# Edge stage's first microseconds: VectorE converts the row numbers first, ScalarE clears the sums

## What is computed

```python
h = relu(u[row] + v[col])
mask = sigmoid(h @ W2 + b2)
sum_w[row]  += mask                 # segment sums over the edges
sum_wx[row] += mask * x[col]
agg = sum_wx / (sum_w + 1e-9)
```

## Time and profile before

| | us |
|---|---|
| time, median of 3 runs | 4230.29 (4230.21 to 4234.32) |
| the profiled execution's own time | 4232.93 |
| its span, first to last instruction | 4231.2 |
| GpSimd's gathers L1706, busy in the span | 1089.1 in 1088 instructions |
| VectorE / TensorE / ScalarE / GpSimd busy in the span | 2994.9 / 3503.2 / 2188.8 / 1547.7 |

### The profile page before, as it was taken

The page is one execution under the profiler, slowest core; times in us unless marked ns, Lnnn a source line. Parts: engine busy times, 40 slices in busy tenths (PEclk is TensorE's granted clock), DMA queues, the critical chain, the costliest instruction groups (busy, mean ns, idle before and its releaser), DMA issues. The chain is left out here.

```text
span 4231.2 us, 94148 instructions
## 1 busy us (share of the span) xinstructions
PE 3503.2 (83%) x20637; PEld 2391.9 (57%) x20638; DVE 2994.9 (71%) x11952; ACT 2188.8 (52%) x6957; POOL 1547.7 (37%) x1256
## 2 busy tenths in 40 slices
PE   5878882698889899995997898688888888888884
PEld 2377772333333344443445344588888888888873
DVE  8899987698888888885003002688888888787875
ACT  2178884266677788884002001455555555555544
POOL 0078874000000000001002001377777777777770
PEclk8855555699999999997999999899999999999996
DMA  2011113001111222221983885355555555555551
GB/s 49 1 11 15 15 17 84 10 35 44 62 70 79 88 97 96 96 90 65 328 303 131 313 304 189 123 151 153 153 151 151 150 150 149 149 150 149 151 147 41
DMA packets 276478, 498.31 MB, mean 118 GB/s; under 512 B 92441, under 2 KB 192944, under 8 KB 276256
## 3 DMA queue, kind: packets, MB, share of 16 engines
q1 hardware_dynamic: 209922, 347.11, 24.4%
q0 software_dynamic: 66336, 149.10, 13.0%
HBM read 391.18 MB, written 104.89 MB: 117 GB/s over the span
## 5 line engine op out<-in xcount | busy, mean ns | idle before, releaser
L1706 POOL DMA_INDIRECT xs<-edge_table,ea_row_stage x1088 | 1089.1, 1001 | 347.4 <-issue 326.1
L1257 PE MATMUL a_agg_ps<-a_adj_ring,parts 128*128 128x512 f16 (+1 forms) x2548 | 523.7, 369 | 46.1 <-DMA a_adj_ring<-adjacency 46.1
L1926 ACT ACTIVATE slot_dst<-ea_onehot,ea_mask 128x128 f32<-128x128 f16 x1632 | 535.7, 399 | 13.2
L1056 PE MATMUL ab_agg_ps<-ab_adj_stage,parts 128*128 128x512 f16 x1911 | 528.2, 387 | 0.0
L1880 PE MATMUL ea_psz<-parts,ea_onehot_t 128*128 x2176 | 309.2, 287 | 206.6 <-issue 188.5
L1920 ACT ACTIVATE ea_mask<-ea_dot,b 128x4 f32<-128x4 f32 x408 | 121.3, 297 | 676.6 <-DVE slot_src L1831 672.9
L441 POOL DMA_INDIRECT records<-both_parts,record_row x98 | 356.1, 3633 | 291.0 <-ACT both_parts L467 269.1
L1397 POOL TENSOR_TENSOR parts<-xs,parts 128x896 f16<-128x896 f32 x7 | 13.2, 1883 | 1225.1 <-ACT parts L1391 1225.1
L1891 PE MATMUL ea_psa<-xs,slot_dst 128*128 128x129 f32 x3264 | 438.6, 278 | 2.4 <-ACT slot_dst L1926 2.4
L1129 ACT ACTIVATE ab_src_off<-iota,ab_neg_src 128x128 f16<-128x128 f16 x712 | 282.2, 396 | 304.8 <-issue 141.2
L1257 PEld LDWEIGHTS a_agg_ps<-a_adj_ring,parts 128*128 128x128 f16 x2548 | 242.2, 98 | 327.8 <-DMA a_adj_ring<-adjacency 47.0
(11 more groups left out here) (391 smaller groups left out, 6455.8 us busy)
## 6 DMA issues: line engine op xcount, KB each, us to landing
a_adj_ring<-adjacency SPq DMA_DIRECT2D x182, 896.0 KB, 4.6
ea_low_rows<-low_rows SPq DMA_DIRECT2D x411, 128.0 KB
adjacency<-ab_adj_stage SPq DMA_DIRECT2D x91, 512.0 KB, 2.6
adjacency<-ab_adj_stage SPq DMA_DIRECT2D x91, 384.0 KB, 2.3
ea_near_rows<-near_rows SPq DMA_DIRECT2D x137, 128.0 KB
xs<-edge_table,ea_row_stage POOLq DMA_INDIRECT x1088
edge_table<-vx SPq DMA_DIRECT2D x12, 512.0 KB, 2.9
ea_row_stage<-row_columns SPq DMA_DIRECT2D x272, 2.0 KB, 1.8
```

The costliest lines, as they stand in the source:

```text
L1056: ins = nc.tensor.matmul(agg_ps[:, :], lhs(r, t), stage[:, k, :], start=start and r == 0, stop=stop and r == parts - 1)
L1257: ins = nc.tensor.matmul(ps[:, h, 0:width], lhs(r, t), ring[:, g % SLOTS, k * DB:k * DB + width], start=t == 0 and r == 0, stop=t == NT - ...
L1706: nc.gpsimd.indirect_dma_start(got[:, h, g, k, 0:ROW], None, m.table, bass.IndirectOffsetOnAxis(ap=row_s[:, h, g, k:k + 1], axis=0)).then_ ...
L1926: ins = nc.scalar.activation(hot_m[:, g, k, :], hot[:, h, g, :, k], ACT.Copy, scale=mask[:, g, k:k + 1])
```

## The change

VectorE now begins with the conversion of the column numbers (L1770 to L1772 of before) and the copies to `row_s`; the two buffers of ones, `lo16` and the wait for `s_ones` come behind the copies, ahead of the first one-hots. The clearing of `m.acc` leaves VectorE: ScalarE writes it as its first instruction of the stage, as a copy of a zero row that is broadcast over the 49 tiles, and that instruction adds the 16 to `s_add`. VectorE's first addition of turn 1 now waits for `s_add` too. `lo16` is followed by a wait for its completion.

```diff
         @block.vector
         def _(dve):
             ch = Chain(dve, s_v)
-            nc.vector.memset(m.acc[:, :, :], 0.0)
-            dve.sem_inc(s_add, 16)
-            nc.vector.memset(near_x[:, :, :], 1.0)
-            nc.vector.memset(got[:, :, :, :, ROW:ROW + 4], 1.0).then_inc(s_ones, 1)
-            nc.vector.tensor_copy(lo16[:, :], m.slot_src[:, 0:SCP])
             ai = m.slot_dst[:, SCP:2 * SCP].bitcast(I32)
             ch(nc.vector.tensor_copy(ai, m.slot_dst[:, 0:SCP]))
             ch(nc.vector.tensor_scalar(ai, ai, SPAN - 1, None, ALU.bitwise_and))
             ch(nc.vector.tensor_scalar(row_of, ai, float(NP - 1), None, ALU.min))
             dve.sem_inc(s_table, 1)
-            dve.wait_ge(s_ones, 2)
...
                 if q == 0:
                     dve.wait_ge(s_agg[g], t)
-                if seen >= 2 or g or q:
-                    dve.wait_ge(s_add, t * 6 + (g * 2 + q + 10))
+                dve.wait_ge(s_add, t * 6 + (g * 2 + q + 10))
...
             stage_rows(base[0:2], 0)
             stage_rows(base[4:6], 1)
+            nc.vector.memset(near_x[:, :, :], 1.0)
+            nc.vector.memset(got[:, :, :, :, ROW:ROW + 4], 1.0).then_inc(s_ones, 1)
+            ch(nc.vector.tensor_copy(lo16[:, :], m.slot_src[:, 0:SCP]))
+            dve.wait_ge(s_ones, 2)
             one_hots(base, 0, 0, 0)
...
+            nc.scalar.activation(m.acc[:, :, :], m.zeros16[:, 0:AW].unsqueeze(1).broadcast_to([P, NT, AW]), ACT.Copy).then_inc(s_add, 16)
             act.wait_ge(s_ones, 2)
             turns(act, step)
```

## The result

| | us |
|---|---|
| the changed kernel, median of 14 runs | 4226.08 (4218.87 to 4231.18) |
| the kernel before, measured beside it, median of 14 | 4232.6 (4224.47 to 4240.76) |
| ratio | 0.9981 (0.9973 to 0.9990), or -8.0 us (-11.4 to -4.2) |
| the profiled execution, and its span | 4226.97, 4225.3 |

The forecast was 4223.0, that is 7.3 us less than the median of the three runs of before that were known then; the measured median lies 3.1 us above it, inside the range. Of these 3.1 us, 2.3 are the kernel before itself, whose median is 4232.6 in 14 runs where it was 4230.29 in three. The medians lie 6.5 us apart, the means 7.9, and the ratio gives 8.0.

What follows compares the result with a forecast made beforehand. GpSimd's unbroken line of gathers bounds the stage, with VectorE's preamble bare ahead of it. 8.03 us of earlier start less 0.7 for lengthened gathers gives 7.3 us, from median 4230.29 to 4223.0; range 4218.8 to 4227.8.

Steps and rivals of the forecast that it cites:

- The line of gathers as the bound: GpSimd issues 1088 gathers one behind another over 1423.2 us; moving the first gather moves the end by as much.
- At a fixed distance: What follows the last gather of the stage was said to follow it at an unchanging distance.
- VectorE's start at 2688.40: VectorE is free at 2688.40, before its memset's row at 2689.68, so L1770 at 2696.43 can start 8.03 us earlier.
- late-start rival: The 1.4 us ahead of VectorE's memset are a real delay that L1770 would suffer too; gain 6.0 us, chance 0.12.
- Kept as it is: 3.14 us: VectorE's conversions L1770 to L1772 keep their 3.14 us; from L1770 to the first gather are 5.52 us.
- The lengthened gathers: VectorE's work beside the first four gathers stretches them from 4.68 to 5.32 us; 0.7 us of loss taken.
- The covers: ScalarE's clearing costs nothing, with 10 us of cover; VectorE's 4.32 us idle before first scores shrinks by about 1 us.
- The sign that would have made the forecast wrong: A gap before a gather of turn 2 showing a releaser other than "issue"; no size of gap given.
- Unlengthened gathers: Rival: the first four gathers run at 0.96 us each; gain 8.9 us, time 4221.4, chance 0.14.
- A new wait before turn 2: Rival: crowded transfers delay landings by 3 us and GpSimd's line stops for 1.5; gain 5.8 us, chance 0.12.
- Another releaser of the first gather: Rival: something other than VectorE's copies released the first gather, only about 1 us moves; 4229 us, chance 0.02.
- Slower through another phase of the loop: Rival: VectorE's one-hots fall on other gathers all loop; at 0.12 us more a turn, 4239.3 us, chance 0.04.

Runs made afterwards that it cites:

- the clearing alone: The kernel before with only the clearing of the sums moved to ScalarE, VectorE's other work in its old order; -6.4 +- 3.2 us against the kernel before.
- order-alone kernel: The changed kernel, but the clearing stays on VectorE, behind the copies and ahead of the first one-hots; -4.5 +- 3.5 us against the kernel before.
- the longer front: The kernel before with the clearing memset done four times, all ahead of the copies; two runs, +12.1 +- 3.5 and +17.4 +- 4.9 us against the kernel before.

## Why the prediction was right

**The line of gathers as the bound.** At the fast pace it held. The first gather's 7.2 us are 7.4 at the 17th and 7.6 at the 65th, and the line's length stayed within 3 us. The time moved by 8.0 (4.2 to 11.4), forecast 7.3. "At a fixed distance" was too strong: from the last gather's start to the end are 106.1 and 103.6 us in the two traces of the kernel before and 106.6 in the changed one.

**VectorE's start at 2688.40, 1.3 us ahead of its row.** Shown three times over: L1765 started 0.02 us after the ramp fill, repeated memsets come 6.71 us apart, and the clearing alone brought 6.2 us with a held-up cast. The late-start rival is out.

**"Kept as it is: 3.14 us" was mis-sized.** I let the three conversions keep their durations though they now ran beside the ramp fill. The first took 2.05 us instead of 1.01. The conversions to the first gather were 6.4 us and not 5.5, and the gain at the first gather 7.2 and not 8.03. I had used the rule on shared access, and looked only at VectorE holding up GpSimd, not at the reverse.

**The lengthened gathers were near in size for a partly wrong reason.** Forecast 5.32 us for four, found 5.11, which is a loss of 0.43 against the 0.7 of the sum (its own terms gave 0.64). The first took 1.85, which I had only as a bound (it began with the cast), and so the second began just as the one-hots ended, and stayed at 0.98 where I had 1.75. Fifth gather: forecast 7.3 us sooner, found 6.8. That the line of before lost another 0.6 us on gathers up to the 17th, which the changed kernel does not, brought it to 7.4. I had no term for that. So the 7.3 was met partly by luck: 0.8 too much for the start, 0.3 too much for the lengthened gathers and 0.6 left out nearly cancel.

**The covers.** The clearing on ScalarE took 5.48 us, forecast 5.47, and nobody waited for it. VectorE still idled for 4.22 us before its first scores, where I had 3.4. Its own first one-hots came only 5.5 us sooner instead of 6.3, and the fourth gather's rows landed later: from that gather's end to the scores are 3.4 us (3.2 in the second trace of the changed kernel), where the kernel before has 2.2 and 2.7. That may be the crowd of transfers, for which I had named up to 1 us; no run separates it. VectorE's idle time hid it.

The sign that would have made the forecast wrong, a releaser other than "issue" before a gather of turn 2, does stand in the trace (the views of GpSimd and of TensorE):

```profile
2720.10 0.96 POOL L1706 DMA_INDIRECT xs<-edge_table,ea_row_stage  x1 [0.30 <-issue]
2721.36 0.96 POOL L1706 DMA_INDIRECT xs<-edge_table,ea_row_stage  x1 [0.30 <-PE ea_psa L1888]
```

```profile
2717.26 1.93 PE L1888 MATMUL ea_psa<-xs,slot_dst 128*128 128x129 f32 x8
```

But the gap is the usual 0.30 us, and it is before the turn's second gather, where the program has no wait; turn 2's first gather shows "issue". So nothing was lost there, and the sign was badly chosen: it should have asked for a longer gap. The spare time before turn 2 did shrink, from 1.8 us to 0.9 (2719.19 to 2720.10).

**The rivals.** Unlengthened gathers: out, by 5.11 and by the order-alone kernel's 3.92, which is what unlengthened looks like. A new wait before turn 2: none that took time at the fast pace; the slow pace has such a wait in nearly every turn, but not through the change, since the kernel before with the longer front has it too. Another releaser of the first gather: out, the copies still release it and it moved by 7.2 us. Slower through another phase of the loop: nothing of it at the fast pace.

The Trainium skill, SBUF — State Buffer, section "Who interferes with whom", says that the engine which issues second is fully blocked by a two-port instruction of VectorE or by GpSimd. The trace roughly agrees for the ramp fill (1.02 us lost to a fill of 1.20) and for the cast (0.83 us to a cast of 0.96). It says, marked as inferred, that a tensor_tensor leaves descriptor writing alone, and also that an instruction with two SBUF inputs holds up a GpSimd instruction that reads SBUF. A gather that begins under L1781, which has two SBUF inputs, loses 0.45 us in two kernels. The measurement decides against the first; it fits the second if the gather's reading of its row numbers is what waits, which no run here shows. For the page alone the prediction put 0.6 us of loss in the first four gathers; from its own rows it is 0.4 to 0.5 (1.92 or 2.02, then 0.96, 1.24 and 0.96, against 4.68), and 0.43 was found.

## What to carry to other kernels

When a stage is one engine's unbroken line of issues, a preamble changes little but its start: find the first instruction of the line, walk back through what released it, and put nothing else in front of that. Before you sum durations of instructions that you move, ask what each will newly run beside on the engine with which it shares access to SBUF, in both directions; here that was worth 1.0 us one way and 0.8 the other. And take a memset's cost from the distance between neighbours, not from its row.

## What the hardware showed unexpectedly

- A VectorE memset's row starts late: 5.33 us shown for 6.6 us of work (6321 elements), 2.62 for 3.2 (3072 of two bytes; 3.33 us from one to the next, with a wait). The missing part appears as "issue" ahead of it. A memset of zeros over 3072 two-byte elements ran as 1536 words, 1.72 us apart; one of ones did not.
- GpSimd's ramp fill, which reads nothing, holds up a VectorE cast that starts beside it: 2.05 us for 1.03.
- One program, two paces, which part only in this stage: the kernel before takes 4231 us or 4651 us, and the changed kernel's traces have 10.46 and 13.5 us a turn, granted clock 0.99 and 0.89 in the loop. At the slow one TensorE stands for about 1 us at a time between matmuls of one run, with no releaser in the profile. The cause stays open.
